# Moving shared-FFN pieces into the attention steps of a one-core cross-attention + MoE kernel, splitting weights in turns, padding from SBUF, and routing in eight batches of two tiles

## The reference

```python
q = ln(x)                                    # per sequence b of 64 tokens
scaled = einsum('bsd,bse->bde', q, ctx) * 256**-0.5
out = einsum('bde,bse->bsd', softmax(scaled, axis=1), ctx)
x = x + out
z = ln(x)
y, g = split(z @ shared_gw.T, 2)             # shared expert, hidden 352
shared = silu(g) * y @ shared_dw.T
scores = sigmoid(z @ gate_w.T)               # 8 experts
idx = top_k(scores + gate_bias, 2); w = scores[idx] / sum(scores[idx])
for e in range(8):                           # routed experts, hidden 176
    g_e, u_e = split(z @ up_w[e].T, 2)
    out += (silu(g_e) * u_e) @ down_w[e].T * w_e
x = x + shared + out
```

## Time and profile before

| what | value |
|---|---|
| median of 3 runs | 275.21 us (273.3 to 276.34) |
| the profiled execution | 275.11 us |
| its span | 273.4 us |
| mean granted TensorE clock | 0.942 |
| busy: PE, DVE, ACT, POOL | 225.7, 182.8, 123.9, 132.3 us |

### The profile page before, as it was taken

One profiled execution on the slowest core, in us unless ns is written; L12 is line 12 of the kernel. 1 busy time (PEld: TensorE's weight loads), 2 busy tenths in 40 slices (PEclk: granted clock), 3 DMA queues, 4 the chain that ended last, 5 costly groups with the idle time before them and its releaser, 6 DMA issues.

```text
span 273.4 us, 5744 instructions
## 1 busy us (share of the span) xinstructions
PE 225.7 (83%) x1597; PEld 198.5 (73%) x1597; DVE 182.8 (67%) x622; ACT 123.9 (45%) x392; POOL 132.3 (48%) x164
## 2 busy tenths in 40 slices
PE   7758888678899956791999679999999999999920
PEld 7446566556587745681899669999899999899810
DVE  2577999999988852510884368777767777613890
ACT  2636666454467621100211175666566666512720
POOL 5346678575677673775000004444544544421791
PEclk9999999797999999786599999999999999999995
...
GB/s 181 273 357 356 291 326 173 38 41 40 55 86 63 64 83 59 104 125 143 83 82 2 0 59 123 122 141 138 136 124 143 122 145 136 58 101 358 327 140 58
DMA packets 24670, 37.27 MB, mean 136 GB/s; under 512 B 5216, under 2 KB 20320, under 8 KB 24128
## 3 DMA queue, kind: packets, MB, share of 16 engines
...
...
## 4 chain that ended last, share of the span: by engine, by line
PE 55%; DVE 21%; issue 9%; POOL 6%; DMA 3%; SPq 2%; ACT 1%; POOLq 1%; DVEq 0%
PE bank L943 10%; PE bank L944 10%; PE bank L945 10%; PE bank L1037 7%; POOL rstd L461 3%; PE bank L1096 3%; PE bank L1114 3%; DMA sul_raw<-shared_upT 3%; DVE nb L678 2%; DVE ve L658 2%; PE bank L1123 2%; DVE x_all L689 2%; PE bank L1128 2%; PE bank L1125 2%; PE bank L1127 2%
## 5 line engine op out<-in xcount | busy, mean ns | idle before, releaser
L507 POOL DMA_INDIRECT expert_out<-att,yi x39 | 37.4, 959 | 77.2 <-ACT att L519 77.2
L448 POOL DMA_INDIRECT slot_rows<-z_all,desti x32 | 31.5, 984 | 12.6 <-issue 8.9
L1056 PE MATMUL bank<-ident 128*128 128x128 f32 x212 | 33.4, 302 | 1.7 <-POOL ident L397 1.7
L1056 PEld LDWEIGHTS bank<-ident 128*128 128x128 f32 x212 | 29.0, 210 | 6.4 <-issue 4.7
L943 PE MATMUL bank<-zTh,suh 128*128 128x256 f32 (+1 forms) x96 | 31.6, 329 | 1.7 <-issue 1.7
L945 PE MATMUL bank<-zTh,sul 128*128 128x256 f32 (+1 forms) x96 | 29.2, 305 | 2.5 <-issue 2.5
L944 PE MATMUL bank<-zTl,suh 128*128 128x256 f32 (+1 forms) x96 | 29.1, 303 | 2.4 <-issue 2.4
L943 PE MATMUL bank<-uph,xh 128*128 x78 | 28.6, 366 | 1.5 <-DVE xl L895 1.1
L545 ACT ACTIVATE att<-bank,nb 128x256 f32<-128x256 f32 x64 | 29.1, 462 | 0.0
L793 DVE SCALAR_TENSOR_TENSOR s_sg<-s_sg,bank 128x256 f32<-128x256 f32 (+1 forms) x16 | 6.7, 416 | 28.9 <-ACT s_sg L529 25.1
L974 PE MATMUL bank<-att,vT 128*64 128x256 f32 x128 | 18.9, 418 | 8.1 <-POOL vT L470 8.0
...
## 6 DMA issues: line engine op xcount, KB each, us to landing
...
```

What stands on the lines that cost most here:

```text
L448: nc.gpsimd.indirect_dma_start(slot_rows, bass.IndirectOffsetOnAxis(ap=desti[:, k, t:t + 1], axis=0), z_all[:, t, :], None).then_inc(sent, 16)
L507: nc.gpsimd.indirect_dma_start(expert_out, bass.IndirectOffsetOnAxis(ap=yi[:, t:t + 1], axis=0), ys[t % 3], None).then_inc(y_out[t % 3], 16)
L1056: mm(warm, ident[:], ident[:], start=first and i == 0, stop=False, skip_group_check=True)
```

## The change

- **Shared pieces inside attention.** Pieces 0 to 5 run in steps 5, 7, ..., 15 on PE and ACT, and one step later on DVE, all through one PSUM bank (`inside_gu`, the bank that `keep_warm` wrote). Pieces 6 to 10 run in steps 16 to 20, pieces 11 to 15 behind them. No filler matmul is left from step 5 on. A down product now stands ahead of the up piece of its number.
- **Weights split by turns.** For expert e, ACT casts the up part in step 3 + 2e and the down part in step 4 + 2e; POOL subtracts the up part in step 4 + 2e, and DVE subtracts the down part (`down_low`) in step 5 + 2e.
- **Pad rows from SBUF.** POOL fills `pad_tile` once; the eight pad DMAs read it instead of DRAM, and only one DRAM tile behind the spare slots is kept instead of eight.
- **The router in eight batches of two tiles**, scores and top in odd steps, pick in even steps, rows in odd steps, and on DVE ahead of `BN_AGGR` and `ve`. Scatters start in step 7. The steps run to 20. `weights` moves from between the pieces to expert step 5.

```diff
-    PADT = SPARE + E
+    PADT = SPARE + 1
...
-    RB = 4
+    BATCHES = [(t, t + 2) for t in range(0, 16, 2)]
...
+        def part_step(r, part):
+            last = BATCHES[r][1] - 1
+            return last + part + (4 if last < NT - GT else 3)
+
+        def batch(p, part):
+            of = [r for r in range(len(BATCHES)) if part_step(r, part) == p]
+            return of[0] if of else None
+
+        def sending():
+
+            at = []
+            for r, (a, b) in enumerate(BATCHES):
+                for t in range(a, b):
+                    at.append(max(part_step(r, 2), at[-1] + 1 if at else 0))
+            return {t: p for t, p in enumerate(at) if p <= NT}
+
+        SEND_STEP = sending()
...
+        INSIDE = 6
+
+        def inside(p):
+            n, odd = divmod(p - 5, 2)
+            return n if 0 <= n < INSIDE and not odd else None
+
+
+        def after(p):
+            return INSIDE + p - NT if NT <= p < STEPS.stop else None
+
+        REST = range(INSIDE + STEPS.stop - NT, PAUSE)
...
+        DOWNS = {n: [] for n in PIECES}
+        for t in range(NT):
+            n = SC * (t // GT) + t % GT + SC + 1
+            DOWNS[max(n, INSIDE) if t < GT else n + (1 if n < INSIDE + GT + 1 else 0)].append(t)
...
         def splitting(p):
-            e = p - FIRST_SPLIT
-            return e if 0 <= e < LAST else None
-
-
-        def ahead(p):
-            return p - NT if p in AHEAD else None
-
+            e, odd = divmod(p - FIRST_SPLIT, 2)
+            return (e if 0 <= e < LAST else None), odd
...
             def pad_experts():
 
-                sp.wait_ge(pads_in, 32)
+                sp.wait_ge(pad_row, 5)
                 sp.wait_ge(count_done, 1)
                 for e in range(E):
                     at = sp.value_load(padrow[0:1, e:e + 1], min_val=0, max_val=E * REG - P)
-                    t = E * REG + (SPARE + e) * P
-                    sp.dma_start(slot_rows[bass.ds(at, P), :], slot_rows[t:t + P, :]).then_inc(pads_out, 16)
+                    sp.dma_start(slot_rows[bass.ds(at, P), :], pad_tile[:, :]).then_inc(pads_out, 16)
 
             pad_experts()
             sp.wait_ge(sc_done, B2 * NT)
             sp.wait_ge(sent, 16 * K * NT)
+            sp.wait_ge(pads_in, 32)
             sp.wait_ge(pads_out, 16 * E)
...
+            def make_pad():
+                nc.gpsimd.memset(pad_tile[:, 0:D], 0.0).then_inc(c_pool, 1)
+                nc.gpsimd.memset(pad_tile[:, D + 1:ROW], -1.0).then_inc(c_pool, 1)
+                n_pool[0] += 2
+                pool.wait_ge(c_pool, n_pool[0])
+                iota(pad_tile[:, D:D + 1], [[0, 1]], TRASH + SPARE * P, 1).then_inc(pad_row, 2)
+
...
-                if splitting(p) is not None:
-                    expert_low(splitting(p))
-                if sending(p) is not None:
-                    scatter(sending(p))
-
-            for t in range(SENT_AHEAD, NT):
+                if p == 1:
+                    make_pad()
+                e, odd = splitting(p)
+                if e is not None and odd:
+                    expert_low(e)
+                for t in range(NT):
+                    if SEND_STEP.get(t) == p:
+                        scatter(t)
+
...
+            def expert_high(e, down):
+                act.wait_ge(ew_in[e // 2], 32)
+                if down:
+                    copy(dnh[:, e, :], dn_raw[:, e, :]).then_inc(dn_high, 1)
+                else:
+                    copy(uph[:, e, :], up_raw[:, e, :]).then_inc(up_high, 1)
+
...
                     normalised(p)
-                if ahead(p) is not None:
-                    shared_piece(ahead(p))
-            for n in range(len(AHEAD), PAUSE):
+                e, odd = splitting(p)
+                if e is not None:
+                    expert_high(e, odd)
+                if inside(p) is not None:
+                    shared_piece(inside(p))
+                if after(p) is not None:
+                    shared_piece(after(p))
...
-            def expert_high(e):
-                dve.wait_ge(ew_in[e // 2], 32)
-                nc.vector.tensor_copy(uph[:, e, :], up_raw[:, e, :]).then_inc(ew_high, 1)
-                nc.vector.tensor_copy(dnh[:, e, :], dn_raw[:, e, :]).then_inc(ew_high, 1)
+            def down_low(e):
+                dve.wait_ge(dn_high, e + 1)
+                nc.vector.tensor_tensor(dnl[:, e, :], dn_raw[:, e, :], dnh[:, e, :].bitcast(F32),
+                                        ALU.subtract).then_inc(dn_low, 1)
...
+            def routing(p):
+
+                r = batch(p, 2)
+                if r is not None:
+                    rows(r)
+                r = batch(p, 0)
+                if r is not None:
+                    n_top[r] = route_scores(r)
+                r = batch(p, 1)
+                if r is not None:
+                    route_pick(r, n_top[r])
 
             def statistics(p):
                 marks = []
@@ -826,13 +874,17 @@
                     n_2 = stats_2(p - 1)
                 if live(p - 3):
                     z_low(p - 3)
+                if p < NT:
+                    routing(p)
+                    e, odd = splitting(p - 2)
+                    if e is not None and not odd:
+                        down_low(e)
...
                 if 0 <= p < DC:
                     shared_high(p)
-                if splitting(p) is not None:
-                    expert_high(splitting(p))
                 if p == 1:
                     dve.wait_ge(const_done, 8)
-                if ahead(p) is not None:
-                    shared_piece(ahead(p))
-                r = batch(p, LAG_SCORE)
-                if r is not None:
-                    n_score[r] = route_scores(r)
-                r = batch(p, LAG_TOP)
-                if r is not None:
-                    n_top[r] = route_top(r, n_score[r])
-                r = batch(p, LAG_PICK)
-                if r is not None:
-                    route_pick(r, n_top[r])
-                r = batch(p, LAG_ROW)
-                if r is not None:
-                    rows(r)
-            for r in range(routed(LAG_PICK), NT // RB):
-                if r >= routed(LAG_SCORE):
-                    n_score[r] = route_scores(r)
-                if r >= routed(LAG_TOP):
-                    n_top[r] = route_top(r, n_score[r])
-                route_pick(r, n_top[r])
-            for n in range(len(AHEAD), PAUSE):
+                if inside(p - 1) is not None:
+                    shared_piece(inside(p - 1))
+                if p >= NT:
+                    routing(p)
+                    e, odd = splitting(p - 2)
+                    if e is not None and not odd:
+                        down_low(e)
+                if after(p) is not None and after(p) > INSIDE:
+                    shared_piece(after(p) - 1)
+            pad_rows()
+            for n in range(REST.start - 1, PAUSE):
                 shared_piece(n)
-                if n == len(AHEAD):
-                    for r in range(PLACED, NT // RB):
-                        rows(r)
-                    pad_rows()
-                if n == len(AHEAD) + 2:
+                if n == REST.start - 1:
                     slot_table()
-                if n == len(AHEAD) + 4:
-                    weights()
...
+                if s == LATE_SPLIT + 3:
+                    weights()
...
-                for t in range(r * RB, (r + 1) * RB):
+                for t in range(*BATCHES[r]):
...
+                if n == INSIDE:
+
                     pe.wait_ge(exp_done, B2 * NT)
-                if n >= 3:
+                if 1 <= n < INSIDE:
+                    pe.wait_ge(shm_done, n)
+                if n >= INSIDE + 3:
                     pe.wait_ge(shm_done, n - 2)
                 if c == 0:
...
                 pe.wait_ge(shm_done, SC * (g + 1))
                 if t == 0:
                     pe.wait_ge(sd_in, 16)
+                    pe.wait_ge(exp_done, B2 * NT)
+                if t == 1:
+
+                    pe.wait_ge(shm_done, INSIDE)
...
-                r = batch(p, LAG_ROW)
-                if r is not None:
-                    ranks(r)
-                if live(p):
+                if inside(p) is not None:
+                    shared_piece(inside(p))
+                elif live(p) and p < 5:
                     keep_warm(FILL)
                 if live(p - 3):
                     route_logits(p - 3)
                 if live(p - 2):
                     z_T(p - 2)
-                if ahead(p) is not None:
-                    shared_piece(ahead(p))
+                if after(p) is not None:
+                    shared_piece(after(p))
+                r = batch(p, 1)
+                if r is not None:
+                    ranks(r)
                 if live(p):
-                    keep_warm(FILL_Z)
                     attend(p)
-            for n in range(len(AHEAD), PAUSE):
+            for n in REST:
                 shared_piece(n)
-                if n == len(AHEAD):
-                    for r in range(PLACED, NT // RB):
```

(1 more changed line is left out.)

99 lines of the change are left out of this document (45 added, 54 removed).

## The result

The changed kernel takes **279.03 us** (median, 276.94 to 279.62), the kernel before 274.73 beside it: a ratio of 1.014, 95% interval 1.009 to 1.0195. It is 1.4% slower, where 260.0 and 251 to 273 were forecast. The profiled execution has a span of 277.8 us.

What follows compares the result with a forecast made beforehand. Attention was taken as a loop through POOL, DVE and PE, the stretch behind as pieces, downs and waiting, the experts as PE-bound. 275.1 + 7.6 + 2 - 25.2 + 0.5 = 260.0 us, range 251 to 273.

Steps and rivals of the forecast that it cites:

- Attention: Loop from `rstd` of step 3 to that of step 16: 79.7 us against 72.1, +7.6, from router and `down_low` work.
- +2 for the clock: In attention, PE idles ahead of attend in odd steps and drops to half speed: 0 to 7 us, taken as +2.
- Eight pads in 10.4 us: Between attention and experts, SP issues eight pad DMAs at 1.3 us each, 10.4 in all.
- Between attention and experts, -25.2: Stretch from `rstd` of step 16 to the first expert transpose: 33.2 us against 58.4 before, a gain of 25.2.
- PE reaches the last ranks ... X + 14.3: Behind attention, PE reaches the last ranks 14.3 us after X, `rstd` of step 16, with about 0.8 of waiting for pick.
- 29.7, and 2 for waits: PE's own work between attention and experts, 29.7 us plus 2 of waits; the other chain was said to decide.
- the bound of 41: Upper bound for the stretch between attention and experts, 41 us, if the odd stretch of PE gaps and slow pads returns.
- Rival 1: Between attention and experts, PE gaps and slow pad issue return as pads and last scatters overlap: +6.2, 266 us; chance 0.20.
- Experts and tail, +0.5: `weights`, some 2 us of DVE, enters the PE-bound expert stage: 0 to 1 us, taken as +0.5.
- Rival 2: Without filler PE's low clock stays through attention, a pair of steps takes about 18 us for 12.8: 287 us; chance 0.07.
- the prediction's own signs of being wrong: Attention ends after 115, the pads take 17 us again, or the stretch to the experts keeps over 40.

Runs made afterwards that it cites:

- f: The changed kernel with filler matmuls again from step 5 on ahead of attend, and at the start of steps 17 to 20: 279.1 us, 1.028 of before.
- b: The kernel before with one wait more: SP issues the eight pad DMAs only when all 32 scatters have landed; ratio 0.998 to before.
- k: The changed kernel, but POOL waits ahead of tile 14's scatters until the 28 scatters before have landed: 276.4 us, 1.041 of before.
- c: The changed kernel, but behind attention TensorE makes a batch's ranks ahead of that step's shared piece and downs: 275.3 us, 1.014 of before.
- i: The changed kernel, but each shared piece goes ahead of the down products of its number on TensorE: 264.5 us, 0.998 of before.
- e: The changed kernel with router work in VectorE's free slot in attention, and ranks ahead of pieces behind attention: 269.7 us, 0.997 of before.
- j: The changed kernel with three edits: router work in VectorE's free slot, ranks ahead of pieces behind attention, piece ahead of downs: 260.3 us, 0.982 of before.

## Why the prediction was wrong

- **Attention** (+7.6, +2 for the clock): right. `rstd` of step 16 came at 107.65, +9.4; the loop itself grew 8.7. The five pairs took 13.0, 13.7, 12.3, 12.9 and 12.5, 64.4 in all (`rstd` of steps 5 to 15: 38.82 to 103.23), against 64.0 without the clock; steps 3 to 6 took 17.7 against 16.3. Rows measured 0.72 and scores with top 1.46, against 0.94 and 1.65; no `ve` was stretched; filler that lifted the clock gained 2.3 (f).
- **Eight pads in 10.4 us**: 10.49, by luck. The price, 1.3, is that of a copy from DRAM, and b's eight took 10.22 us with it; from `pad_tile` a pad is 1.1 us, and eight take 8.5 to 9.3 where there is no stall. The stall made up the difference.
- **Between attention and experts, -25.2**: failed; -7.8, since the stretch was 50.6 and not 33.2. Two steps of it. "PE reaches the last ranks ... X + 14.3" was X + 23.8: PE waited 5.1 us on the way where 0.8 stood, and four downs and four pieces took 15.3 where 10.8 stood, part of them at half speed (a clock term, +2, was given to attention and none to this stretch). And "29.7, and 2 for waits" for PE alone was 50.6: it, not the pads, ended last. The runs split the 17.4 us that were missing into three parts, each read from one or two traces.
  - *The stall*, 4.3: 46.3 us of stretch in k, 46.2 in c, which had none. ACT's start 4.2 us late at 141.03 is the same amount. Why it is there in one trace and not in another is open.
  - *The order*, 6.3: 40.0 in i against 46.3 in k (10.1 between e and j). It is the one part of the change that the prediction described and gave no price: the down ahead of the piece of its number. A down needs what VectorE makes of the piece just finished, or the add that frees its bank, and nothing stood in between.
  - *What is left*, 6.8: with the order undone and no stall the stretch is 40.0, within the bound of 41 that the prediction set for another case, and not 33.2. In i the last ranks still come at X + 22.0 (128.84), where four pieces and four downs take 16.4 us and the waits 2.6, at a mean granted clock of 0.71. From there on the forecast was near: `pad_rows` 2.3 us behind them (3.3 stood), the eight pads in 8.65 (10.4), the first transpose 5.7 behind the pads (about 5). So PE at half speed and waiting, ahead of the last ranks, is the rest; no run takes the two apart, since f's filler fills PE too. SP's queue and PE's timeline of i:

```profile
128.84 0.17 PE L1040 MATMUL bank<-both,below 128*128 128x8 bf16 x1
...
132.38 8.65 SPq L375 DMA_DIRECT2D slot_rows<-pad_tile  x8
```

- **Rival 1** (the odd stretch comes back, +6.2): it came, and cost 4.3 us. Of PE's wait of 5.98 us that ends with it the order would have made 1.8 anyway (1.81 in c and k). Its mechanism, pads beside scatters, was wrong (b).
- **Experts and tail, +0.5**: +2.7. 1.2 of it lies up to the end of the last expert scatter (85.7 us before, 86.9 after, from the first transpose; the experts now begin at half speed). The rest lies in the tail and was not followed up; other executions of the changed kernel and its variants have 118.2 to 121.0 there, of the kernel before and its variants 116.8 to 118.6.
- **Rival 2** (slow through attention, 287) did not happen: the clock came back each time, and its mean in the loop was 0.86. The slower side came by a mechanism that was no rival.

The total: 275.1 + 9.4 - 7.8 + 2.7 = 279.4; the profiled execution took 279.6. Of the prediction's own signs of being wrong, one came true: the stretch kept over 40.

The one part that is shown to pay by itself is the turns (-1% alone). j, with all parts and the three edits, beats the kernel before by 1.8%; it was not timed beside the changed kernel. What its small batches and its pieces inside attention add to the turns was not measured alone.
